# Hybrid attention block: state products interleaved with the inner read-outs, value projection moved ahead, value copy moved ahead

## The reference, cut to what matters

```python
q = phi(x @ W_q); k = phi(x @ W_k); v = x @ W_v      # phi = elu + 1, 64 columns each
def step(carry, inp):
    S, z = carry
    S = S + k_t[:, :, None] * v_t[:, None, :]
    z = z + k_t
    o_t = einsum('bij,bj->bi', S, q_t)
    denom = max(sum(z * q_t), 1e-06)
    return (S, z), o_t / denom
x = x + attention(layernorm(x)) @ W_o
```

## Time and profile before

| | us |
|---|---|
| median of 3 runs | 346.27 |
| lowest, highest | 344.2, 346.51 |
| the profiled execution, device time | 345.94 |
| its span, first to last instruction | 344.1 |
| mean granted TensorE clock over the span | 0.948 |

### The profile page before, as it was taken

The page is one execution under the profiler, slowest core; times in us unless marked ns, Lnnn a source line. Parts: engine busy times, 40 slices in busy tenths (PEclk is TensorE's granted clock), DMA queues, the critical chain, the costliest instruction groups (busy, mean ns, idle before and its releaser), DMA issues.

```text
span 344.1 us, 7662 instructions
## 1 busy us (share of the span) xinstructions
PE 295.8 (86%) x2177; PEld 257.4 (75%) x2177; DVE 243.3 (71%) x1012; ACT 182.8 (53%) x545; POOL 210.9 (61%) x244
## 2 busy tenths in 40 slices
PE   7999999899976599999998997888885599999970
PEld 7566666675866599999964885766875599999970
DVE  4878998878761577777726998889573368777750
ACT  3765555321854376667613752634663376676730
POOL 4954487886485455655545857788575536565560
PEclk9999999989996899999999998999996889999995
DMA  7999211002323443221108001112313344221000
GB/s 195 257 332 144 34 40 33 31 32 58 73 63 88 94 92 91 65 57 32 32 11 236 1 1 33 40 39 71 81 41 86 93 89 104 73 55 41 31 8 1
DMA packets 32521, 25.64 MB, mean 75 GB/s; under 512 B 6000, under 2 KB 28785, under 8 KB 32480
## 3 DMA queue, kind: packets, MB, share of 16 engines
q1 hardware_dynamic: 27328, 16.51, 21.0%
q0 software_dynamic: 4576, 8.54, 7.5%
q10 hardware_dynamic: 576, 0.10, 0.2%
HBM read 14.57 MB, written 11.53 MB: 76 GB/s over the span
## 4 chain that ended last, share of the span: by engine, by line
PE 54%; POOL 10%; DVE 10%; issue 8%; ACT 6%; another core or an unknown queue 6%; DMA 1%; POOLq 0%; ACTq 0%; SPq 0%; DVEq 0%
PE pair L1498 18%; PE pair L1484 13%; POOL sorted L490 6%; PE bank L1484 6%; PE bank L1474 3%; DVE stats L797 2%; POOL rows L464 2%; PE pair L1358 2%; PE pair L1311 2%; ACT hT L741 2%; PE pair L1322 2%; PE pair L1277 1%; PE pair L1350 1%; PE pair L1333 1%
## 5 line engine op out<-in xcount | busy, mean ns | idle before, releaser
L1498 PE MATMUL pair<-w2s,hT 128*128 x624 | 87.0, 285 | 1.4 <-issue 1.1
L490 POOL DMA_INDIRECT sorted<-rows,place x64 | 67.5, 1055 | 28.2 <-issue 20.1
L1498 PEld LDWEIGHTS pair<-w2s,hT 128*128 128x128 f32 x624 | 79.6, 200 | 1.9 <-issue 1.6
L1146 DVE SCALAR_TENSOR_TENSOR ys<-pair,xs 128x128 f32<-128x128 f32 x78 | 27.3, 350 | 53.2 <-PE pair L1498 29.5
L1484 PE MATMUL pair<-xsT,w1s 128*128 128x128 f32 x432 | 61.3, 280 | 1.3 <-ACT xsT L736 1.3
L503 POOL DMA_INDIRECT x_mid<-ys,xs x39 | 41.2, 1056 | 33.2 <-DVE ys L1146 31.1
L503 POOL DMA_INDIRECT out<-ys,xs x39 | 41.1, 1055 | 33.2 <-DVE ys L1146 30.4
L1484 PEld LDWEIGHTS pair<-xsT,w1s 128*128 128x128 f32 x432 | 55.4, 196 | 2.1 <-issue 0.9
L736 ACT COPY xsT<-bank 128x128 f32<-128x128 f32 x78 | 20.8, 267 | 64.0 <-issue 34.1
L660 ACT COPY w1s<-w1all 128x516 f32 x78 | 49.5, 635 | 3.0 <-DVE etab L1074 1.9
L1484 PE MATMUL bank<-xsT,w1s 128*128 128x128 f32 x192 | 30.6, 294 | 12.9 <-ACT xsT L736 12.5
(11 more groups left out here) (164 smaller groups left out, 495.0 us busy)
## 6 DMA issues: line engine op xcount, KB each, us to landing
xs<-sorted SPq DMA_DIRECT2D x78, 66.0 KB
w1all<-in_L_ffn_W_b SPq DMA_DIRECT2D x8, 258.0 KB
rows<-in_L_attn_a_x SPq DMA_DIRECT2D x8, 256.0 KB, 4.1
w2s<-in_L_ffn_W SPq DMA_DIRECT2D x8, 256.0 KB, 6.5
rows<-x_mid SPq DMA_DIRECT2D x8, 256.0 KB, 4.3
sorted<-pad SPq DMA_DIRECT2D x30, 66.0 KB, 3.5
sorted<-rows,place POOLq DMA_INDIRECT x64
x_mid<-ys,xs POOLq DMA_INDIRECT x39
```

The lines of the kernel that those rows point to most:

```text
L490: pool.indirect_dma_start(sorted_rows[l], bass.IndirectOffsetOnAxis(ap=place[:, t:t + 1], axis=0), rows[:, t, :], None).then_inc(s_sent[l] ...
L1146: nc.vector.scalar_tensor_tensor(out=ys[b][:], in0=bank[6 + i % 2][:, 0:P], scalar=xs[b][:, GATE:GATE + 1], in1=xs[b][:, 0:D], op0=ALU.mul ...
L1498: mm = nc.tensor.matmul(bank[6 + i % 2][:, 0:P], hT[i % NB][:, c], w2s[:, bass.ds(e, 1), c, :].rearrange("p o d -> p (o d)"), start=(c == ...
```

## The change

On TensorE, scores and turned keys become one function, `score_and_turn`: after the second score product come the waits that stood ahead of the turned keys (the last copy of keys and values, and the relu of the next group, `rel`), then each further score product is followed by one turned key. The turned values follow as before. In slot 1 the set-up transposes now come behind all of these, where they stood between the scores and the turned keys.

`project_v(k)` moves from the end of the slot to right behind the transposes of x. `updates` and `read_intra` become one function, `updates_and_intra`, which takes all of its waits at its head (the copy `kv`, the old state, `am`, the old copy of the output) and then alternates the two kinds of products. The count of group k-3 moves from ahead of the state products to behind this function. On ScalarE `evac_v(k)` moves ahead of `evac_o(k-1)`. No operation is added or removed, and no amount of data changes.

```diff
@@ -685,9 +685,9 @@
                     row_veps(AS, k - 2)
                 if k + 2 < NG:
                     norm(AS, k + 2)
+                evac_v(k)
                 if 0 <= k - 1:
                     evac_o(k - 1)
-                evac_v(k)
 
             def gates_of_mix(g):
                 act.wait_ge(BS["mix"], g + 1)
@@ -1277,50 +1277,57 @@
                 nc.tensor.matmul(bank[2][0:VC, :], wc[:, 2 * H:3 * H + E], xnT[g % 2][:], start=True, stop=True
                                  ).then_inc(AS["vp"], 1)
 
-            def score(g):
+            def score_and_turn(g):
                 p = g % 2
+
+                def turn_k(j):
+                    t = slice(j * P, (j + 1) * P)
+                    nc.tensor.transpose(bank[1][:, j * H:(j + 1) * H], qk[p][H:P, t], ident[H:P, H:P])
+
                 pe.wait_ge(AS["phi"], g + 1)
                 pe.wait_ge(AS["v"], g + 1)
                 after(pe, AS["am"], g)
                 for j in range(GT):
                     t = slice(j * P, (j + 1) * P)
                     last = nc.tensor.matmul(bank[4][:, t], vT[p][0:H, t], qk[p][0:H, t], start=True, stop=True)
-                last.then_inc(AS["scores"], 1)
-
-            def turn_kv(g):
-                p = g % 2
-                pe.wait_ge(AS["phi"], g + 1)
-                pe.wait_ge(AS["v"], g + 1)
-                after(pe, AS["kv"], g)
-
-                pe.wait_ge(AS["rel"], min(g + 2, NG))
-                for j in range(GT):
-                    t = slice(j * P, (j + 1) * P)
-                    nc.tensor.transpose(bank[1][:, j * H:(j + 1) * H], qk[p][H:P, t], ident[H:P, H:P])
+                    if j == GT - 1:
+                        last.then_inc(AS["scores"], 1)
+                    if j == 1:
+                        after(pe, AS["kv"], g)
+
+                        pe.wait_ge(AS["rel"], min(g + 2, NG))
+                    if j >= 1:
+                        turn_k(j - 1)
+                turn_k(GT - 1)
                 for j in range(GT):
                     t = slice(j * P, (j + 1) * P)
                     last = nc.tensor.transpose(bank[3][:, j * VC:(j + 1) * VC], vT[p][:, t], ident[0:VC, 0:VC])
                 last.then_inc(AS["kvT"], 1)
 
-            def updates(g):
+            def updates_and_intra(g):
                 p = g % 2
                 n = GT if p == 0 else GT - 1
+
+                def intra(j):
+                    t = slice(j * P, (j + 1) * P)
+                    nc.tensor.matmul(bank[5][H:P, t], kv[p][:, j, VC:KC], am[:, j], start=(j == 0), stop=False,
+                                     skip_group_check=True)
+
                 pe.wait_ge(AS["kv"], g + 1)
                 after(pe, AS["state"], g)
-                for j in range(n):
-                    last = nc.tensor.matmul(bank[5][0:H, H * j:H * n].rearrange("v (i k) -> v i k", k=H),
-                                            kv[p][:, j, 0:H], kv[p][:, j:j + 1, VC:KC].to_broadcast([P, n - j, H]),
-                                            start=(j == 0), stop=(j == n - 1))
-                last.then_inc(AS["upd"], 1)
-
-            def read_intra(g):
-                p = g % 2
                 pe.wait_ge(AS["am"], g + 1)
                 after(pe, AS["oe"], g)
                 for j in range(GT):
-                    t = slice(j * P, (j + 1) * P)
-                    nc.tensor.matmul(bank[5][H:P, t], kv[p][:, j, VC:KC], am[:, j], start=(j == 0), stop=False,
-                                     skip_group_check=True)
+                    if j == 1:
+                        intra(1)
+                    if j < n:
+                        last = nc.tensor.matmul(bank[5][0:H, H * j:H * n].rearrange("v (i k) -> v i k", k=H),
+                                                kv[p][:, j, 0:H], kv[p][:, j:j + 1, VC:KC].to_broadcast([P, n - j, H]),
+                                                start=(j == 0), stop=(j == n - 1), skip_group_check=True)
+                    if j == n - 1:
+                        last.then_inc(AS["upd"], 1)
+                    if j != 1:
+                        intra(j)
 
             def read_inter(g):
                 p = g % 2
@@ -1368,10 +1375,9 @@
                 if k - 2 >= 0:
                     project_out(k - 2)
                 if 0 <= k - 1:
-                    score(k - 1)
+                    score_and_turn(k - 1)
                     if k == 1:
                         setup_transposes()
-                    turn_kv(k - 1)
                 if k == 0:
                     turn_output_weights()
                 if k + 1 < NG:
@@ -1382,19 +1388,19 @@
 
                     pe.wait_ge(s_w2, 16 * (1 + E))
                     keep_clock(2)
+                if k < NG:
+                    project_v(k)
+                if 0 <= k - 1:
+                    updates_and_intra(k - 1)
                 if 3 <= k < NG:
 
                     pe.wait_ge(AS["xnew"], k - 1)
                     count(AS, k - 3, attn_counts)
                 if 0 <= k - 1:
-                    updates(k - 1)
-                    read_intra(k - 1)
                     read_inter(k - 1)
                 if k == NG:
                     pe.wait_ge(AS["xnew"], k - 1)
                     count(AS, k - 3, attn_counts)
-                if k < NG:
-                    project_v(k)
 
             def mix_to(g, j):
                 return mix_pair[g % 2][:, j // 2, 2 * P * (j % 2):2 * P * (j % 2 + 1)]
```

## The result

The changed kernel takes 358.33 us (median of 4 runs, 357.58 to 360.54), the kernel before beside it 345.6 us (4 runs, 344.2 to 346.51). The ratio is 1.037, with a 95% interval from 1.033 to 1.041: 12.7 us slower. The execution that was profiled took 360.54 us with a span of 358.7, which is 14.6 us more than the span of the kernel before. The forecast was 351, range to 355: the sign was right, the size was less than half of the measured one, and the time lies above the range.

A forecast was written before the change was run, and what follows sets the result against it. VectorE's chain was taken to bound attention (92% of the time), nearly balanced with TensorE. 7.11 - 4.28 + 0.2 + 0.6, less 0.1 for the last read-outs, gave +3.5; clock drops 1.5; so +5.0 on 345.94: 351 us, range 346.5 to 355.

The forecast's parts named there:

- rival 5: After attention: the delay is partly taken up by later waits or the experts' first stage, +0 to +3 us; chance 0.15.
- The price of the handover: Slots 2 to 7: VectorE idles behind `am` for state products, 0.97 us with three, 1.40 with four, together 7.11.
- One costs from nothing to 1.0 us; I take half: Slots 4 to 8: about three drops of TensorE to half clock in place of one, 1.5 us in all.
- these waits vanish, and TensorE comes 1.3 us early: Attention slots: VectorE no longer waits for `dmax`; all 4.28 us of its old waits are replaced by 7.11.
- `dmax` still waiting for the output projection: New profile, attention: listed as a sign of being wrong, since `dmax` was to have no waits from slot 3 on.
- Rival 3: Attention and tail: a clock drop in nearly every slot, half of the handovers at 1.2 GHz, +8.5 us, 354.5; chance 0.07.
- Slot 8 has the six table steps, which cover it: Slot 8, VectorE: table steps behind `am` hide the wait for state products; cost nothing, some 0.97 us without that cover.
- The old waits: Slots 2 to 7: VectorE's present waits, 4.28 of 52.81 us, all go, including what half clock cost in slot 7.
- if all of the late start stays: Slot 1: scores waiting for `rel` and late set-up transposes delay `dmax` by 0.6 us, bounds 0 and 1.2.
- The count: Slots 4 and 6: `placed(k-3)` ends about 0.1 us after VectorE wants it, 0.2 together; covered with four products.
- Rival 4: Attention: TensorE is the bound after all, so the change is faster, 345.9 - 2.9 = 343 us; chance 0.08.
- Rival 2: Attention: the handover costs as forecast but no more clock drops come, +3.5 us, 349.4; chance 0.20.

The follow-up runs named there:

- h3: Kernel before with one more wait for `am`, ahead of the state products, repeating e2 with more rounds; 327.98 us against 317.27, ratio 1.031.
- h2: Changed kernel, old order of scores, set-up transposes and turned keys, seven useless products before the `am` wait (now last), no `keep_clock`; 324.01 us, ratio 1.020.
- g1: Changed kernel with the wait for `am` as the last of its four waits, where it stood third; one run, 355.66 us.
- f1: The changed kernel itself, no line different, run again beside the kernel before; 330.17 us against 317.45, ratio 1.043.
- h1: Changed kernel without the two useless `keep_clock` products of slot 8; 332.16 us against 317.27, ratio 1.046.
- f4: Kernel before with scores and turned keys alternating and the set-up transposes behind them; 321.04 us against 317.45, ratio 1.011.
- g3: Kernel before with scores and turned keys alternating from slot 2 on, slot 1 in the old order; 343.7 us against 343.67, ratio 0.999.
- f3: Kernel before with only the count of group k-3 moved behind the state products and inner read-outs; 323.33 us, ratio 1.018.
- e1: Changed kernel with the state products ahead of the wait for `am` and the inner read-outs behind it; 322.62 us, ratio 1.012.
- e2: Kernel before with one more wait for `am`, ahead of the state products; 331.32 us against 318.64, four runs, no interval.
- set g: One of four sets of follow-up kernels, each run beside the kernel before on the same chip; there the kernel before took 343.67 us.
- g4: Kernel before with early value projection and value copy, and in slot 8 one table step ahead of `state` instead of two; 345.06 us against 343.67, ratio 1.002.
- sets e, f and h: The other three sets of follow-up kernels, each beside the kernel before on the same chip, which took 318.64, 317.45 and 317.27 us.

## Why the prediction was right in sign and wrong in size

The terms of the sum against the same terms of the profiled execution, in us:

| term | forecast | measured | from |
|---|---|---|---|
| slot 2 begins later | +0.6 | +2.12 | 25.70 - 23.58 |
| handover in slots 2 to 7, full clock | +7.11 | +8.12 | 1.14 + 1.13 + 1.14 + 3 x 1.57 |
| half clock in slots 2 to 7 | +1.5 | +3.83 | 2.43 and 2.69 less 1.57 each, and 1.16 + 0.69 at `dmax` |
| old waits that are gone | -4.28 | -4.28 | |
| VectorE's own work, the count | +0.2 | +0.63 | 61.11 - 11.95 - 48.53 |
| slot 8 and the tail | -0.1 | +3.60 | 10.68 - 7.08 |
| sum | +5.0 | +14.0 | |

*That VectorE's chain sets the time of attention, and that it now waits for products behind `am`: right.* Slots 2 to 7 less their waits are 49.16 us against 48.53. (The 0.41 us before `dmax` at 66.41, for which the earlier trace rows names no engine, was read as the output projection's; its products, 65.28 + 1.10, ended 0.03 us before.) The experts' first row moved by 14.0 us (85.02 to 99.04) and the span by 14.6: nothing was given back later, and rival 5 fell. h3 shows the one wait as the main cause, with nothing else changed: 3.1% by itself, of the 3.7 to 4.3% of the whole change.

*The price of the handover: right for another program than this one.* The 0.97 and 1.40 us worked out from the earlier trace rows are what h2 has (0.96, 1.40). The changed kernel has 1.14 and 1.57. The step left out that the diff puts one more wait behind the one for `am`; g1 puts it last and sheds 0.11 us, and with TensorE busy up to the wait (h2) the rest goes as well. That makes 1.0 us in all, a small miss.

*"One costs from nothing to 1.0 us; I take half": the step that failed most.* Three drops were forecast in slots 4 to 8, and there were three in slots 2 to 8, beside slot 1's. But a drop does not end with the slot it is in: 6.6 and 13.4 us in a row, against the 3.3 of the earlier trace rows from which I took the price. Its cost has three places, the state products (0.86 and 1.12 more), the output projection (0.69 and 1.16), and slot 8, and only the first was priced. The sentence "these waits vanish, and TensorE comes 1.3 us early" is true at full clock only: in h2 no wait for `dmax` is left in slots 2 to 7, in the changed kernel two. `dmax` still waiting for the output projection was one of the forecast's own signs of being wrong. With slot 8 the clock's terms come to 3.83 + 3.60 = 7.4 us, more than the 6 of the forecast's far end, "with a drop in every slot", although there were only three. Rival 3, which put the clock with the tail at 5 us and gave it a chance of 0.07, was nearest. The price hangs on where a drop falls, and 7.4 us is this execution's: in f1 two drops cost 1.29 + 1.32 = 2.6 us. But a drop cost more than the upper bound of 1.0 us in both. For the wait alone, h3 and h2 leave 9.9 - 5.6 = 4.3 us to the clock, an estimate; added up from h3's rows it is 0.67 + 3.69 + 2 x 1.09 = 6.5. Either is near half of that kernel's loss.

*"Slot 8 has the six table steps, which cover it": true at full clock, and again the clock was left out.* In f1 the cover held: `state` did not wait and slot 8 took 7.07 us. I looked at what VectorE has between `am` and `state`, and not at what TensorE has ahead of the state products: two useless products. At full clock they end at 87.85 in f1, before `am` does (88.32); at half clock, in the result's profile, they end at 92.95 and the cover is long used up. h1 shows that taking them away does not help.

*The old waits, "-4.28": right for the execution of the earlier trace rows only.* In f4, which from slot 2 on differs from the kernel before by the alternation alone, slots 2 to 7 hold 1.09 + 0.42 + 0.42 = 1.93 us of waits and no half clock. They took 50.46 us there and 60.05 in f1, 9.6 more, against 61.11 - 52.81 = 8.3 in the result. So f1 loses as much as the result does although its clock costs less: that the two ratios are so close may be in part chance.

*Slot 1: the right mechanism, mis-sized.* The upper bound of 1.2 us, "if all of the late start stays", was too low by 0.9. I moved `rwoT` to 17.8 and it started at 17.61. What was missing is that TensorE waited in the middle of its scores, 1.17 us, and then fell to half clock for 3.3 us, in which the value projection took 1.91 us where it takes 1.02 or 1.08 at full clock. In f4 this part alone costs 3.5 us, and in g3, without slot 1, nothing.

*The count, "0.2 us": about right in this program, by the cover of the handover.* Alone it costs 5.6 us (f3), and with the products ahead of the wait it comes back at once (e1). It was worth a rival: whoever repairs the handover alone uncovers it.

*The value projection: right that TensorE gains and VectorE hides it,* but not quite nothing: alone it takes 1.4 to 1.7 us off the program, as it removes waits for the output projection.

*Rival 4, TensorE as the bound,* fell with e2 and h3. The page of the Trainium skill named there ("TensorEngine Tiling (Array Packing)", Theoretical Speedup) gives up to twice the speed, and this trace agrees: the two halves did run beside each other. State products and read-outs of slot 3 start in pairs, at 39.27 and 39.28, 39.51 and 39.55, and are all done in 1.28 us, against 1.30 and 1.0 us for the two kinds one after the other. Only TensorE's time was saved by that, and it had time to spare. Rival 2, no more drops, fell with the four stretches at 0.50.

The other page of the Trainium skill that the prediction named, "TensorE: Matmul & The Clock Gate", Part 3, has matmuls strictly in order in start and end. The starts of slot 3 go against it, as those of the earlier trace rows do: the second record of the first state product starts at 39.51, behind the first of the read-out that follows it in the program (39.28). No term of the sum hung on this.

## What to carry to other kernels

Before a wait is moved up on an in-order engine, ask which engine will stand still for what is now behind it, and price that from the end of the awaited work to the end of the products; then put the latest wait last. An idle stretch of the matrix engine has a second price, its clock: count every place that reads its output until the clock is back, the stage's end included. Useless work that keeps the clock up doubles as well (1.93 to 3.71 us here), and the engine can fall to half clock without it (h1), so price it both ways. One profile shows one place for the drops and another execution of the same program another (f1): do not read a mechanism out of a single slot. And take a change of several parts apart: here one part was 0.5% faster and three lost, one of them in a single slot and one hidden by another.

## What the runs showed of the hardware beside that

ScalarE can start late on work that is ready. In slot 5 of the kernel before the turned values end at 50.38, and the copy of keys and values starts at 51.11:

```profile
49.91 0.47 PE L1302 MATMUL bank<-ident,vT 72*128 72x72 f32 x4
...
51.11 0.37 ACT L636 COPY kv<-pair 128x256 f32<-128x256 f32 x1 [1.91 <-PE bank L1302]
```

That is 0.73 us late. In the profile of before the delay is 0.42, 0.73, 0.47 and 0.65 us in slots 4 to 7, in the result's profile of the changed kernel 0.53 in slots 5 and 7, and in three kernels of set g up to 1.37 (g4; in g1 it is 0.03 to 0.04 throughout). In all twelve kernels of sets e, f and h it is 0.03 to 0.05 in each of the eight slots. In g4 ScalarE also stands idle among the experts, where the profile names nothing on this core that it waits for:

```profile
100.00 0.23 ACT L609 ACTIVATE le<-ld 128x32 f32<-128x32 f32 x1 [3.32 <-issue]
...
113.31 0.27 ACT L736 COPY xsT<-bank 128x128 f32<-128x128 f32 x1 [4.94 <-remote]
```

The late starts come in the result's runs and in set g, in which the kernel before took 344 to 346 us and not 317 to 319. What holds ScalarE is not shown, and no run here was made for it. It matters for the forecast: in f4, with all copies on time, slots 2 to 7 hold 1.93 us of waits and no drop of the clock, so the 4.28 us, and the drop of the earlier trace rows, seem to come in part from these late starts. In the changed kernel the two late copies stand in the two slots in which `state` waited 2.43 and 2.69 us; in f1, with all copies on time, the two drops in slots 2 to 8 began in slots 4 and 6 and cost less. That the late copies moved them is not shown. Whether the early value projection keeps its gain under them is open as well.
